# Context projections split into 128 and 64 rows, the scan's inputs on another engine, and maxima spread anew

## What is computed

```python
x = x + cross_attention_0(layernorm(x), ctx)    # 16 heads of 16; q = xn @ Wq + bq, k = ctx @ Wk + bk, v = ctx @ Wv + bv
x = x + state_space(layernorm(x))               # conv, delta, h[t] = exp(delta A) h[t-1] + delta B u, y = C h + D u, y * silu(res)
x = x + experts(layernorm(x))                   # self attention, then 8 gated experts of 1024
x = x + cross_attention_1(layernorm(x), ctx)    # as the first
x = x + linear_attention(layernorm(x))
x = x + grouped_sets(layernorm(x))
```

## Time and profile before

| what | us |
|---|---|
| median of 3 runs (lowest, highest) | 1377.11 (1371.65, 1380.97) |
| the profiled execution, its own time | 1377.1 |
| its span, first to last instruction | 1375.0 |
| PE busy | 1212.0 |
| DVE busy | 715.2 |
| ACT busy | 714.6 |
| POOL busy | 224.6 |

### The profile page before, as it was taken

The page is one execution under the profiler, slowest core; times in us unless marked ns, Lnnn a source line. Parts: engine busy times, 40 slices in busy tenths (PEclk is TensorE's granted clock), DMA queues, the critical chain, the costliest instruction groups (busy, mean ns, idle before and its releaser), DMA issues.

```text
span 1375.0 us, 29487 instructions
## 1 busy us (share of the span) xinstructions
PE 1212.0 (88%) x12749; PEld 779.0 (57%) x12749; DVE 715.2 (52%) x1351; ACT 714.6 (52%) x995; POOL 224.6 (16%) x118
## 2 busy tenths in 40 slices
PE   8799999999999989316799989999999999989566
PEld 6256666566655656216598345666565666656344
DVE  2546555455555553568223526555555555555342
ACT  3246666666666657242213346666666666657322
POOL 0222222222222200033000212222222111210000
PEclk9689999999999999657799779999999999999769
DMA  8969777767776680610804969777777777790440
GB/s 150 138 82 123 94 93 95 99 84 97 98 96 91 76 174 3 208 64 0 306 1 76 131 84 118 97 95 97 97 90 97 92 99 102 82 151 7 170 159 5
DMA packets 80947, 138.18 MB, mean 100 GB/s; under 512 B 9064, under 2 KB 72176, under 8 KB 80304
## 3 DMA queue, kind: packets, MB, share of 16 engines
q1 hardware_dynamic: 79920, 136.16, 63.5%
q10 hardware_dynamic: 896, 0.12, 0.1%
HBM read 57.96 MB, written 0.15 MB: 42 GB/s over the span
## 4 chain that ended last, share of the span: by engine, by line
PE 73%; DVE 17%; DMA 4%; issue 2%; ACT 2%; POOL 0%; SPq 0%; ACTq 0%; DVEq 0%; POOLq 0%
PE ring L543 39%; PE st L543 17%; PE ot L543 15%; DVE mpart L1221 8%; DMA qst<-rowb 4%; DVE arena L1348 2%; PE ring L674 1%; DVE arena L1352 1%; ACT arena L932 1%; PE ring L549 0%; DMA warena<-ctxT 0%; PE ring L642 0%; DVE work L1342 0%; POOL arena L532 0%; DVE work L1296 0%
## 5 line engine op out<-in xcount | busy, mean ns | idle before, releaser
L1221 DVE TENSOR_REDUCE mpart<-ring 128x1 f32<-128x448 f32 x896 | 516.5, 620 | 441.5 <-PE ring L543 439.4
L955 ACT ACTIVATE work<-st 128x1024 f32<-128x1024 f32 x392 | 400.8, 1022 | 199.5 <-PE st L543 195.3
L543 PE MATMUL ring<-arena,qst 96*128 96x448 bf16 x896 | 300.5, 370 | 4.9 <-DVE mpart L1221 1.9
L543 PE MATMUL st<-qst,arena 97*128 97x128 bf16 x3136 | 244.7, 221 | 22.2 <-DMA qst<-rowb 21.1
L543 PE MATMUL ot<-work,arena 128*17 128x128 f32 x6272 | 250.3, 277 | 8.5 <-issue 6.4
L543 PEld LDWEIGHTS st<-qst,arena 97*128 97x128 bf16 x3136 | 198.5, 98 | 86.9 <-DMA qst<-rowb 32.8
L543 PEld LDWEIGHTS ot<-work,arena 128*17 128x17 f32 x6272 | 138.6, 97 | 150.9 <-issue 104.0
L495 POOL TENSOR_TENSOR arena<-arena 128x896 f32<-128x896 f32 x52 | 98.1, 1887 | 720.9 <-ACT arena L928 720.9
L543 PE MATMUL ring<-warena,wkv 96*128 96x448 f32 x448 | 195.8, 567 | 2.0 <-DVE mpart L1221 1.3
L543 PE MATMUL ring<-wkv,warena 96*128 96x256 f32 x784 | 192.8, 389 | 1.1 <-DVE mpart L1221 1.0
L543 PEld LDWEIGHTS ring<-wkv,warena 96*128 96x128 f32 x784 | 149.4, 194 | 29.1 <-DVE mpart L1221 11.0
(11 more groups left out here) (278 smaller groups left out, 624.9 us busy)
## 6 DMA issues: line engine op xcount, KB each, us to landing
arena<-arena SPq DMA_DIRECT2D x336, 224.0 KB, 11.3
warena<-ctxT SPq DMA_DIRECT2D x28, 672.0 KB, 13.4
arena<-ffn_W SPq DMA_DIRECT2D x16, 1024.0 KB, 12.4
arena<-f SPq DMA_DIRECT2D x2, 4096.0 KB, 24.3
arena<-scratch_bc SPq DMA_DIRECT2D x1, 2048.0 KB, 7.1
arena<-rows SPq DMA_DIRECT2D x1, 1792.0 KB, 7.0
warena<-w_in_proj SPq DMA_DIRECT2D x1, 1024.0 KB
warena<-w_W SPq DMA_DIRECT2D x1, 1024.0 KB, 13.8
```

Source lines behind the costliest of these rows:

```text
L543: return nc.tensor.matmul(o, l, r, start=start, stop=stop, **kw)
L955: nc.scalar.activation(pbuf[:, n % 2], st[:, 2 * (n % 2):2 * (n % 2) + 2].rearrange("p b k -> p (b k)"), ACT.Exp).then_inc(*signal(f"{lay} ...
L1221: V.reduce_max(mpart[:, 2 * h + hf:2 * h + hf + 1], ring[:, BANKS[step][0], 0:HALF], AX_X).then_inc(*signal(f"{lay}_b_max"))
```

## The change

- The 192 inputs of a projection are cut into 128 and 64 rows (`TAIL`). The first matmul has 128 rows. The second has 64, and its operands lie in partitions 0 to 63 and, as a copy, in 64 to 127: the 64-row matmuls of one bank use the lower half of the array's rows, those of the neighbouring bank the upper half, and they are issued in turn, behind the 128-row ones of both banks.
- The projections come in pairs of steps: values 0 and 1 in unit 0, 2 and 3 in unit 2; keys 0 and 1 in unit 5, 2 and 3 in unit 7. Both steps of a pair are signalled at the second's end.
- A chunk's context and the projection weights are loaded by three transfers each (128 rows, and the 64 twice).
- `per_unit`: 19 maxima in the first nine units from the second chunk on, 13 in the last five. In the first chunk 32 and 13.
- State space: dBu is computed on DVE, one block ahead, and not on POOL. The gate's sigmoid is no longer ahead of the convolution's: its addition and first half of the reciprocal stand behind the copies of x_dbl, the second half behind `sp_u`, its product behind the first dBu.

```diff
-    plan = [("k", 0, 0), ("k", 0, 1), ("k1", 0, 0), ("k", 0, 2), ("k2", 0, 0), ("k", 0, 3), ("k1", 0, 1), ("k2", 0, 1)]
+    plan = [("k", 0, 0), ("k", 0, 1), ("k1", 0, 0), ("k", 0, 2), ("k", 0, 3), ("k2", 0, 0), ("k1", 0, 1), ("k2", 0, 1)]
     plan += [("v", 0, n) for n in range(4)] + [("k", 1, n) for n in range(4)] + [("v", 1, n) for n in range(4)]
     plan += [("k1", 1, 0), ("k1", 1, 1), ("k2", 1, 0), ("k2", 1, 1)]
-    plan += some(2 * H, 0) + [("row", 0, 0)] + [("k", 2, n) for n in range(3)] + score(0) + [("k", 2, 3)] + score(1)
-
-    values = {u: u for u in range(4)}
-    keys = {5: 0, 6: 1, 7: 2, 8: 3}
+    plan += some(2 * H, 0) + [("row", 0, 0)] + [("k", 2, n) for n in range(2)] + score(0) + [("k", 2, n) for n in range(2, 4)] + score(1)
+
+    values = {0: (0, 1), 2: (2, 3)}
+    keys = {5: (0, 1), 7: (2, 3)}
     firsts, seconds = {7: 0, 9: 1}, {10: 0, 11: 1}
     for c in range(NCH):
-        per_unit = ((4,) * 8 + (0,) if c == 0 else (1, 1, 1, 1, 3, 2, 2, 2, 2)) + (3, 4, 3, 4, 3)
+        per_unit = ((4,) * 8 + (0,) if c == 0 else (1, 3, 1, 3, 3, 1, 3, 1, 3)) + (3, 2, 3, 2, 3)
         for u in range(UNITS):
             if c + 2 < NCH and u in values:
-                plan.append(("v", c + 2, values[u]))
+                plan += [("v", c + 2, n) for n in values[u]]
             if c + 3 < NCH and u in keys:
-                plan.append(("k", c + 3, keys[u]))
+                plan += [("k", c + 3, n) for n in keys[u]]
             plan.append(("pv", c, u))
...
                 load(wx[:, 0], chunked(a[f"{lay}_wq"]), f"{lay}_wq_in")
-                for n in range(2):
-                    load(wkv[:, :, n], a[f"{lay}_wkv"][n].rearrange("(k p) n -> p k n", p=CP), f"{lay}_wkv_in")
+                load(wkv[:, 0], a[f"{lay}_wkv"][:, 0:P].rearrange("n p d -> p n d"), f"{lay}_wkv_in")
+                for part in range(2):
+                    load(wkv[part * TAIL:(part + 1) * TAIL, 1], a[f"{lay}_wkv"][:, P:CC].rearrange("n p d -> p n d"),
+                         f"{lay}_wkv_in")
                 load(wx[:, 1], chunked(a[f"{lay}_wo"]), f"{lay}_wo_in")
             def load_ctx(lay, par, at):
-                load(ctxt[0:CP, par], a["ctxT"].rearrange("(k p) n -> p k n", p=CP)[:, :, bass.ds(at, CK)],
-                     f"{lay}_ctx_in{par}")
+                load(ctxt[:, par, 0], a["ctxT"][0:P, at:at + CK], f"{lay}_ctx_in{par}")
+                for part in range(2):
+                    load(ctxt[part * TAIL:(part + 1) * TAIL, par, 1], a["ctxT"][P:CC, at:at + CK],
+                         f"{lay}_ctx_in{par}")
...
             attention("L0")
-            pool.wait_ge(*done_of("dtu_ready"))
-            pool.wait_ge(sem("bc_in"), 16)
-            for b in range(NB):
-                if b >= 2:
-                    pool.wait_ge(sem("scanned"), b - 1)
-                nc.gpsimd.tensor_tensor(
-                    m_["dBu"][:, b % 2].rearrange("p (n t) -> p n t", n=NS),
-                    m3["dtu"][:, b:b + 1].broadcast_to([P, NS, TOK]),
-                    m_["bc"][:, 0:NS * TOK].rearrange("p (n t) -> p n t", n=NS), ALU.mult).then_inc(*signal("dBu_ready"))
             pool.wait_ge(*done_of("ffn_done"))
             attention("L1")
...
                         if n == 0:
-                            pe.wait_ge(sem(f"{lay}_ctx_in{c % 2}"), 16 * (c // 2 + 1))
-                        project(ring[:, bank, 0:HALF], lambda k: wkv[:, k, 0, m * P:(m + 1) * P],
-                                lambda k: ctxt[0:CP, c % 2, k, hf * HALF:(hf + 1) * HALF], f"{lay}_k_full", 2)
+                            pe.wait_ge(sem(f"{lay}_ctx_in{c % 2}"), 16 * PROJECTION_LOADS * (c // 2 + 1))
+                        mm(ring[:, bank, 0:HALF], wkv[:, 0, 0, m * P:(m + 1) * P],
+                           ctxt[:, c % 2, 0, hf * HALF:(hf + 1) * HALF], stop=False, skip_group_check=True)
+                        if hf:
+                            for half, rows_of in enumerate(TAILS):
+                                last = mm(ring[:, BANKS[(kind, c, n - 1 + half)][0], 0:HALF],
+                                          wkv[rows_of, 1, 0, m * P:(m + 1) * P],
+                                          ctxt[rows_of, c % 2, 1, half * HALF:(half + 1) * HALF], start=False,
+                                          skip_group_check=True)
+                            last.then_inc(sem(f"{lay}_k_full"), 2)
                     if kind == "v":
                         for t in range(2 * n, min(2 * n + 2, TPC)):
-                            last = project(ring[:, bank, (t % 2) * D:(t % 2 + 1) * D],
-                                           lambda k: ctxt[0:CP, c % 2, k, t * P:(t + 1) * P],
-                                           lambda k: wkv[:, k, 1, :], None, 2)
-                        last.then_inc(*signal(f"{lay}_v_full"))
+                            mm(ring[:, bank, (t % 2) * D:(t % 2 + 1) * D], ctxt[:, c % 2, 0, t * P:(t + 1) * P],
+                               wkv[:, 0, 1], start=(t % 2 == 0), stop=False, skip_group_check=True)
+                        if n % 2:
+                            for t in (2 * n - 2, 2 * n, 2 * n - 1, 2 * n + 1):
+                                if t < TPC:
+                                    rows_of = TAILS[t // 2 % 2]
+                                    last = mm(ring[:, BANKS[(kind, c, t // 2)][0], (t % 2) * D:(t % 2 + 1) * D],
+                                              ctxt[rows_of, c % 2, 1, t * P:(t + 1) * P], wkv[rows_of, 1, 1],
+                                              start=False, skip_group_check=True)
+                            last.then_inc(sem(f"{lay}_v_full"), 2)
                     if kind == "b":
                             pe.wait_ge(sem(f"{lay}_qst_in"), 16 * SLOTS)
-                        mm(ring[:, bank, 0:HALF], qst[0:CP, 0, h], kst[0:CP, c % KBUFS, h, hf * HALF:(hf + 1) * HALF]
+                        mm(ring[:, bank, 0:HALF], qst[0:STACKED, 0, h], kst[0:STACKED, c % KBUFS, h, hf * HALF:(hf + 1) * HALF]
                            ).then_inc(*signal(f"{lay}_b_full"))
...
-                dve.wait_ge(*done_of("res_exp"))
-                sigmoid_of_exp(m2["sres"])
-                link(V.tensor_tensor(m2["sres"].rearrange("p b t -> p (b t)"), pb[1][:, :],
-                                     m2["sres"].rearrange("p b t -> p (b t)"), ALU.mult))
                 dve.wait_ge(*done_of("xc_exp"))
...
                 V.tensor_copy(m_["bcT"][RANK:RANK + 2 * NS], pb[2][RANK:RANK + 2 * NS, 0:TOK]).then_inc(*signal("bcT_ready"))
+                dve.wait_ge(*done_of("res_exp"))
+                link(V.tensor_scalar(m2["sres"], m2["sres"], 1.0, None, ALU.add))
+                V.reciprocal(m2["sres"][:, 0:NB // 2], m2["sres"][:, 0:NB // 2])
...
                 dve.wait_ge(*done_of("sp_u"))
+                link(V.reciprocal(m2["sres"][:, NB // 2:], m2["sres"][:, NB // 2:]))
...
                 V.tensor_tensor(m3["dtu"], m3["z"], m2["xi"], ALU.mult).then_inc(*signal("dtu_ready"))
+                dve.wait_ge(*done_of("dtu_ready"))
+
+                def inputs(b):
+                    V.tensor_tensor(m_["dBu"][:, b % 2].rearrange("p (n t) -> p n t", n=NS),
+                                    m3["dtu"][:, b:b + 1].broadcast_to([P, NS, TOK]),
+                                    m_["bc"][:, 0:NS * TOK].rearrange("p (n t) -> p n t", n=NS), ALU.mult
+                                    ).then_inc(sem("dBu_ready"), 1)
+
                 def gated(b):
...
+                dve.wait_ge(sem("bc_in"), 16)
+                inputs(0)
+                link(V.tensor_tensor(m2["sres"].rearrange("p b t -> p (b t)"), pb[1][:, :],
+                                     m2["sres"].rearrange("p b t -> p (b t)"), ALU.mult))
                 for b in range(NB):
...
                                     ).then_inc(sem("weighted"), 1)
+                    if b + 1 < NB:
+                        inputs(b + 1)
                     dve.wait_ge(sem("weighted"), b + 1)
                         gated(b - 1)
```

More of the change, by code:

```diff
@@ L33 @@
 CC = 192
-CP = 96
+TAIL = CC - P
 H = 16
@@ L41 @@
 SLOTS = 6
+STACKED = SLOTS * HD
 VW = 32
@@ L50 @@
 EARLY = 3
+PROJECTION_LOADS = 3
 EPS = 1e-5
@@ L252, in build @@
         wx = sb("wx", [P, 2, 2, D])
-        wkv = sb("wkv", [CP, 2, 2, D])
-        qst = sb("qst", [CP + 1, 2, H, TOK], BF16)
+        wkv = sb("wkv", [P, 2, 2, D])
+        qst = sb("qst", [STACKED + 1, 2, H, TOK], BF16)
         qparts = sb("qparts", [P, 3, KC, TOK], BF16)
@@ L373, in build @@
         FREE = {"row": ("row_out", 1), "v": ("v_out", 4), "o": ("o_added", 1), "b": ("b_max", 2 * H), "k": ("k_out", 4)}
+        TAILS = (slice(0, TAIL), slice(TAIL, P))
         AHEAD = {"row": 0, "v": 0, "o": 1, "b": 0, "k": 0}
@@ L415, in attention_loads @@
                 sp.wait_ge(sem(f"{lay}_ones_set"), 1)
-                load(arena[CP:CP + 1, A_KST:A_V].rearrange("p (n k) -> p n k", k=HALF), ones, f"{lay}_ones_in")
```

(23 more changed lines are left out.)

1 line of the change is left out of this document (removed).

## The result

| kernel | median us (lowest, highest), runs | ratio, 95% interval |
|---|---|---|
| before | 1376.96 (1371.65, 1380.97), 4 | |
| changed | 1454.38 (1447.74, 1458.38), 4 | 1.056 (1.0505 to 1.0615) |

The change makes the kernel 5.6% slower, 77 us. The forecast was 1332. The profiled execution of the changed kernel took 1447.7 us (span 1445.6).

What follows compares the result with a forecast made beforehand. PE was taken to bound the kernel, busy 88% of the span. From 1377.1 us, projections -41, maxima -5, layer starts +8 and state space -7.5 gave 1331.6, stated as 1332; range 1306 to 1370.

Steps and rivals of the forecast that it cites:

- the one on the maxima: Steady chunks, maxima moved from 15/17 to 19/13: 0.2 us a chunk gained, 5 us in all, bounds -10 and +19.
- (b): Projection tail bursts: row halves run one after the other, 23 us slower instead of 41 faster, 1396 us; chance 0.12.
- (a): Projection tails: halves overlap only as a staircase, 20 us gained for 41, 1353 us; chance 0.15.
- f: Projection tails: overlap as part of the full saving, total 1377 + 18.5 - 64 f, deciding the sign at 0.29.
- Rival (e): Steady chunks: tails overlap but the row's chain and DMA take the gain, 1365 to 1377 us; chance 0.08.
- Projections: Steady chunks: keys 1.0 us less in 22 chunks, values 0.8 less in 24, 41 us gained.
- Start of each layer: First part of both layers: larger context loads delay the first row, +4 us a layer, +8, bounds 0 and +14.
- State space: Block between the layers: gate's sigmoid off the path and all scans at 4.42 us, 7.5 us gained, bounds 3 and 11.

Runs made afterwards that it cites:

- e_stack_waits: Changed kernel with SP holding the stack's transfers back until the row's transfer is issued, ACT's order kept; 1351.33 us, ratio 0.9828.
- e_casts_moved: Changed kernel with ACT's first cast at unit 6 instead of 7, second casts at 11 and 12 instead of 10 and 11; 1332.13 us, ratio 0.9702.
- e_row_first: Changed kernel with ACT's row copy and transfer moved ahead of the second cast in unit 10; 1342.73 us, ratio 0.9758.

## Why the prediction was wrong, step by step

**The step that failed is the one on the maxima**, taken as a gain of 5 us and bounded at a loss of 10 and a gain of 19. It saw the row's chain ("copy on ACT at 329.59, scores at 331.56 ... 2.0 us that shorter units in front leave more exposed") and priced it as 0.2 us of exposure. What it missed is that the transfer's own time was not fixed. Its 1.6 us held only while it stood ahead of the stack's transfers, and the margin was 0.32 us. The margin is in the timeline of before, just below the copy that rows 4 quote: 329.87 and 330.19. The prediction rests on neither row; of SP's queue it weighed the context loads and wrote "nothing". A unit made shorter by 0.55 us was enough. The transfer became 2.9 us longer and the slow clock behind the wait cost some 3 us more: 5.8 us in a chunk, in 11 chunks of a layer. 22 x 5.8 = 128 us is above what the runs give, though: e_stack_waits, which changes nothing but the order, is 103 us faster (its steady stretches 101 us shorter: 416.0 and 412.4 for 466.7 and 462.5), 4.7 us a chunk. In place of the 5 us gained the step lost some 100. Without that loss the kernel stands at 1351, 19 us above the forecast; they are in what follows.

**The rival with the other sign**, (b), named the wrong place. The halves overlap in full, so (b) and (a) fall: its f is 2.5/2.8 = 0.9 by the chunks and 1 by the slots. The whole kernel gives 52/65 = 0.8. Rival (e) had the right object, "the row's chain and DMA take the gain", but stopped at the gain and gave it 0.08. The range to 1370 ended there as well.

**Projections**, -41: right in PE's own time, not on the clock on the wall. Keys of two steps now take 2.69 us on the chain, where a step took 1.75 before: 2 x (3.50 - 2.69) = 1.6 us a chunk (forecast 1.0). The values' bursts, 3.17 to 3.33 and 2.89 with two maxima of 0.19 each, make 5.3 to 5.5 for 6.0: 0.5 to 0.7 (forecast 0.8). PE's busy time per chunk fell by 2.2, forecast 1.8. The difference in the keys: 12 slots are 4.51 us and the two bursts take 5.38. Of the 0.87 between, each burst's start has 0.25, as each step had before (1.75 for 1.50), which leaves 0.19 for an entry into the halves (priced at 0.25). And four starts became two, 0.5 us that the sum had left out: 1.5 + 0.5 - 0.4 = 1.6.

**The gain of a chunk then reaches the clock on the wall only in part.** In e_casts_moved the two steady stretches are 18.5 and 14.3 us shorter than before (402.1 and 403.6 for 420.6 and 417.9), 33 us for a forecast of 46 with the maxima. Chunks at the full pace gain 2.3 us; others, 34.1 to 38.7 long between row copies, still have waits. The longest in each layer, 37.5 and 38.7 us, are explained by the same race: in the first chunk of the loop that has a stack, e_casts_moved issues the row 1.17 and 0.65 us behind it, the transfer takes 4.2 and 5.4 us, and PE waits 3.0 and 4.2. The rest were not followed up.

The sum also had no term for the meeting of DVE's minimum with POOL's product. It is in the changed kernel too (20 of 28 minima longer than 0.3 us), hidden behind the larger loss. With the order mended and this left, in e_row_first, the two steady stretches are only 3.6 and 8.0 us shorter than before, in a profile of its slowest run.

**Start of each layer**, +8: wrong in sign. To the second row copy it is 6.1 us shorter in the changed kernel, 4.5 in e_casts_moved. The second layer's is shorter too: from its first row copy to its second 51.5 us for 57.2. The first row's transfer took 9.05 us for 12.48, though more was loaded. This number scatters: in the nine kernels with the new loads it is 8.3 to 12.4 us, in the five with the old ones 12.4 to 12.6, and shorter each time in the second layer's start as well (9.1 to 11.3 for 12.5 to 12.7). The stretch shows the rate: in the first 70 us of the changed kernel the traffic is 159 GB/s at a DMA share of 0.94,

```profile
0.00:70.00 70.00, 54.99 (x202) 26.31 (x203) 26.54 (x56) 22.59 (x37) 10.70 (x11) 0.83 0.94 159
```

against 144 at 0.99. The term took bytes times the old rate, and the loads of 128 partitions ran at a higher one. That the partitions are the reason is likely and was not tested by itself.

**State space**, -7.5 with bounds of 3 and 11: right. Alone it gave 9 us. All four scans are 4.42 or 4.43 us as forecast; two of them in the timeline:

```profile
644.51 4.42 DVE L1374 TENSOR_TENSOR_SCAN arena<-arena 128x2048 f32<-128x2048 f32 x1 [1.24 <-ACT arena L1005]
...
653.60 4.43 DVE L1374 TENSOR_TENSOR_SCAN arena<-arena 128x2048 f32<-128x2048 f32 x1
```

That e_casts_moved stands at the forecast's 1332 is partly luck: less from the chunks, more from the starts.

## What to carry to other kernels

A small transfer on the critical path is only as quick as its place among the bulk transfers. Read at its issue which queue issues next and by how many tenths of a microsecond it wins, and treat a change of any unit before it as a change of that race; better, make the order certain. Two swapped lines in the plan widened the margin here to 0.64 us in most chunks, yet the first of a layer could still lose the race; the wait of e_stack_waits held it in all 22. A stretch made shorter on one engine also slides other engines' operations over each other: list the two-operand DVE operations near POOL's, and check after the change whether a short one has grown to end with POOL's. And an edit that loses may hold the larger gain: take it apart before it is dropped.

## What the runs showed of the hardware

- A 4 KB transfer issued behind the first of 12 transfers of another queue (224 KB each as the page of the profile counts them) took 4.2 to 5.7 us, whether it was 0.06 or 1.30 us behind: so in all 22 chunks of three kernels (medians 4.4 to 4.6) and in seven single chunks of four others. Issued 0.17 to 1.46 us ahead of them, it took 1.6 to 1.7 (median of each of eleven kernels), in single chunks up to 3.7. The page "DMA: Bandwidth & Descriptors" of the Trainium skill, section "Queues, rings and completion order", has the engines alternate between queues by packets; it also says that a semaphore's write waits for all earlier writes of its engine, across queues. The trace agrees with both in kind: the row's packets were through 1.1 us later than before, and the landing came 2.0 us behind them for 0.3. That the 1.7 us between is that wait is likely; no run shows it by itself.
- A wait of 3.0 to 4.5 us on PE was followed by a stretch at the lower clock level in all 22 chunks of three kernels, 3.4 to 10.2 us long. In the chunk shown the granted clock is 0.50 for 6.8 us, which costs some 3 us, as much as the gap itself (the chunk's mean of 0.92 over 40.7 us gives 2 x 0.08 x 40.7 = 6.5 us at half speed).
- Two float32 matmuls of 64 rows in different row halves ran side by side from start to end, both records of each: their starts lie 0.007 us apart and their durations are equal (0.640 us, then 0.536), where the next slot comes 0.48 us later.
- DVE's minimum over two operands ended 0.02 to 0.04 us behind POOL's product whenever it had started inside it (medians of 0.82 and 1.34 us for 0.18); a reduction of one operand kept its 0.19.
